# Two parts of an x transform run back to back, and the next layer's second half of products after them

## The reference

```
for i in range(4):
    x1 = _fourier_layer(v, W1, W2)      # rfft2, 24 x 12 modes mixed over 32 channels, irfft2
    x2 = einsum('bcxy,cd->bdxy', v, w_w[i]) + w_b[i]
    v = x1 + x2
    v = (v - mean) * rsqrt(var + eps) * bn_g + bn_b    # mean, var over images and pixels
    if i < 3: v = relu(v)
out = einsum('bcxy,cu->bxyu', v, q_w) + q_b
```

## Time and profile before

| | us |
|---|---|
| median of 3 runs (1403.99, 1404.17, 1419.41) | 1404.17 |
| the profiled execution | 1414.87 |
| its span, first to last instruction | 1413.1 |
| PE busy | 1179.3 |
| DVE busy | 874.0 |
| ACT busy | 540.1 |

### The profile page before, as it was taken

The page is one execution under the profiler, slowest core; times in us unless marked ns, Lnnn a source line. Parts: engine busy times, 40 slices in busy tenths (PEclk is TensorE's granted clock), DMA queues, the critical chain, the costliest instruction groups (busy, mean ns, idle before and its releaser), DMA issues.

```text
span 1413.1 us, 40446 instructions
## 1 busy us (share of the span) xinstructions
PE 1179.3 (83%) x18183; PEld 675.8 (48%) x18183; DVE 874.0 (62%) x1036; ACT 540.1 (38%) x781; POOL 358.5 (25%) x513
## 2 busy tenths in 40 slices
PE   3659899999969999899996998889898877964597
PEld 3434455555544455455554444455455453224562
DVE  6547477677648557576664856657756662058664
ACT  1125345445434434444443543444444462010150
POOL 6382242020326313202032621320202251100000
PEclk9779799999989999999998999999999998985788
DMA  6259998897516999999972699999988065932001
GB/s 158 58 159 222 247 287 202 211 222 185 143 46 181 225 325 366 323 324 319 343 213 62 170 231 328 351 321 308 327 287 273 19 250 200 396 135 51 2 0 31
DMA packets 160086, 300.28 MB, mean 213 GB/s; under 512 B 32552, under 2 KB 104632, under 8 KB 142980
## 3 DMA queue, kind: packets, MB, share of 16 engines
q1 hardware_dynamic: 137754, 254.78, 59.8%
q0 software_dynamic: 19904, 42.18, 10.8%
q10 hardware_dynamic: 2256, 0.75, 0.2%
HBM read 147.86 MB, written 128.48 MB: 196 GB/s over the span
## 4 chain that ended last, share of the span: by engine, by line
PE 63%; DVE 12%; DMA 9%; ACT 6%; issue 4%; SPq 4%; POOL 0%; ACTq 0%; DVEq 0%
PE ps L1589 15%; PE ps L1628 12%; PE ps L1651 7%; PE ps L1663 7%; PE ps L1552 4%; PE ps L1519 4%; PE ps L1614 3%; PE ps L1530 3%; SPq L1045 2%; DMA arena<-half_inverse 2%; DMA maps<-arena 1%; ACT arena L1404 1%; PE ps L1505 1%; DVE ps L1879 1%; DMA half_inverse<-arena 1%
## 5 line engine op out<-in xcount | busy, mean ns | idle before, releaser
L1079 POOL DMA_DIRECT2D arena<-arena x207 | 121.4, 594 | 545.4 <-ACT arena L1421 544.2
L1628 PEld LDWEIGHTS ps<-arena 48*128 48x128 f32 x3072 | 191.9, 198 | 94.6 <-issue 84.1
L1628 PE MATMUL ps<-arena 48*128 48x128 f32 x3072 | 212.6, 290 | 14.6 <-DMA arena<-half_inverse 7.2
L1404 ACT ACTIVATE arena<-ps,arena 128x1024 f32<-128x1024 f32 x96 | 112.3, 1203 | 232.5 <-PE ps L1628 195.0
L1413 ACT ACTIVATE ps<-ps 128x1024 f32<-128x1024 f32 x144 | 145.5, 1011 | 112.1 <-PE ps L1589 111.9
L2035 DVE STREAM_TRANSPOSE arena<-ps 128x1024 f32<-128x1024 f32 x96 | 177.3, 1932 | 1.2 <-PE ps L1651 1.2
L1589 PE MATMUL ps<-arena 32*32 32x512 f32 x2944 | 157.3, 616 | 3.4 <-issue 2.7
L1651 PE MATMUL ps<-arena 32*32 32x512 f32 x3072 | 153.6, 615 | 6.8 <-DVE arena L2022 3.4
L2022 DVE STREAM_TRANSPOSE arena<-arena 128x2048 f32<-128x2048 f32 x64 | 144.1, 2290 | 21.5 <-issue 12.7
L1663 PE MATMUL ps<-arena 128*64 128x96 f32 x2304 | 126.7, 262 | 32.6 <-DVE arena L2035 29.5
L1663 PEld LDWEIGHTS ps<-arena 128*64 128x64 f32 x2304 | 106.9, 145 | 88.3 <-issue 48.6
(11 more groups left out here) (314 smaller groups left out, 1405.3 us busy)
## 6 DMA issues: line engine op xcount, KB each, us to landing
arena<-half_inverse SPq DMA_DIRECT2D x90, 384.0 KB, 10.2
half_inverse<-arena SPq DMA_DIRECT2D x132, 256.0 KB, 4.7
maps<-arena SPq DMA_DIRECT2D x112, 256.0 KB, 4.2
maps<-inputs SPq DMA_DIRECT2D x112, 256.0 KB, 8.9
arena<-maps SPq DMA_DIRECT2D x28, 1024.0 KB, 13.8
maps<-arena SPq DMA_DIRECT2D x28, 1024.0 KB, 9.9
inputs<-maps SPq DMA_DIRECT2D x28, 1024.0 KB, 13.5
arena<-in_mode_w POOLq DMA_DIRECT2D x48, 384.0 KB, 7.1
```

The lines of the kernel that those rows point to most:

```text
L1079: eng.dma_start(dst, src).then_inc((modes_st[batch % 2], last_st, late_st)[part], 16)
L1404: nc.scalar.activation(half(h_out(l, q), h)[:, 1024 * pair:1024 * pair + 1024], ps[:, 2 * pair:2 * pair + 2, :].rearrange("p b n -> p (b n ...
L1628: last = nc.tensor.matmul(ps[:, b, at:at + 128], gtile[s][rows, 4 * b + 2 * h + n, :], iy[rows, :], start=False, stop=(i >= 2 and n == 1))
```

## The change

In each round of a pass TensorE runs the two parts of the x transform one behind the other, and then the second half of the next layer's products. ScalarE copies out in the same order. What is computed is the same.

```
@@ ScalarE
                     if q:
                         modes_evac(l, q - 1, 0)
+                        modes_evac(l, q - 1, 1)
                         square(l, q - 1, 1)
-                        modes_evac(l, q - 1, 1)
@@ TensorE
                     if q:
                         x_transform(l, q - 1, 0)
+                        x_transform(l, q - 1, 1)
                         next_set(l, q - 1, 1)
-                        x_transform(l, q - 1, 1)
```

## The result

The changed kernel took 1468.41 us (median of 4 runs, 1463.93 to 1473.12). The kernel before took 1407.91 us (4 runs). The ratio is 1.042, 95% interval [1.034, 1.049]: 4.2% slower. The forecast was slower, by 42 us; by the ratio it became some 59, and 1468.41 lies above the top of the range (1459). The kernel before was run again beside the experiments and had medians of 1416.74 us (23 runs) and 1414.10 us (17 runs); against these the change costs 52 to 54 us. The profiled execution took 1473.12 us, with a span of 1471.3 us.

What follows compares the result with a forecast made beforehand. The prediction took rounds to be bound by a ring through TensorE and ScalarE's squares. Terms of +47.9, -10 and +4.5 summed to +42.4 us, on the median of 1404.17 a forecast of 1446.6 us, range 1427 to 1459.

Steps and rivals of the forecast that it cites:

- The ring (step 1): Full rounds: TensorE waits for ScalarE's squares, no longer covered by x part 1; +1.14 us in 42 rounds, +47.9 us.
- One term put at nothing: Round q = 15 of each pass: the y transform waits for VectorE's turned map anyway, so the change costs 0.
- rival B: TensorE's clock falls in the new gaps of every round, 2.82 us more each, 118 us in all; 1565 us, chance 0.04.
- Layers 1 and 2 (step 2): Rounds of layers 1 and 2: stops in some 18 of 28 swallow half of the new wait, -10 us.
- the stops: TensorE's instruction supply in layers 1 and 2: standstills without a semaphore, one of 3.79 us, hide new wait, -10 us.
- Rival A: Layers 1 and 2 are paced from outside the round's waits; only layer 0 and pass ends pay, +20.5 us, chance 0.14.
- The end of a pass (step 3): Last round of each pass: ScalarE issues its transfers behind its squares, delaying the mix; +1.5 us each, +4.5 us.

Runs made afterwards that it cites:

- e4: Changed kernel with ScalarE's squares of the second half over one bank of each pair instead of two; 1415.27 us, ratio 1.000 to the kernel before.
- e7: Kernel before with the squares of half 1 over one bank of each pair instead of two; 1395.67 us, measured once.
- e1: Changed kernel with 12 unneeded matmuls (24 rows) added behind the second half of the next layer's products; 1472.79 us, ratio 1.040 to the kernel before.
- e5: Changed kernel with one unneeded matmul of 512 columns (2 rows) behind the second half of the next layer's products; 1451.02 us, ratio 1.025 to the kernel before.
- e9: Kernel before, with ScalarE copying 1024 columns into unread banks before the squares of half 1; 1460.23 us beside 1419.75 for the kernel before, once each.
- e6: Kernel before with the new order on both engines in layers 1 and 2 alone; 1434.78 us, ratio 1.015 to the kernel before.
- e2: Kernel before with the new order on both engines in the last round of each pass alone (q = 16); ratio 0.995 to the kernel before.
- e8: Kernel before with the new order on both engines in the last two rounds of each pass (q = 15 and 16); ratio 0.997 to the kernel before.

## Why the prediction was wrong

- **The ring (step 1) was right in mechanism and near in size.** Forecast 6.72 us from x0 to L1628 and +1.14 a round, measured 6.57 and +0.99. Most of the difference is the pair of x parts: as one row of 48 they take 2.13 us start to start, not 2 x 1.14. Forty-two rounds make 41.6 us instead of 47.9. e4 and e7 show the squares as the cause. One term put at nothing was 0.55 us: in the round with q = 15 the y transform waited for the copy of part 1, which ended 4.76 us after x0 (399.67 + 0.39 - 395.30), 0.10 us before it began, and not for the turned map; the changed kernel gives that back in each pass.
- **The step that failed is the one on the clock, rival B.** I treated it as all or nothing: 1565 us with a chance of 0.04, and nothing for it in the forecast's sum ("the clock of layer 0's window stays at 1.00"). The argument was that gaps of 0.5 us had done nothing and that only 3.83 us had. Between these ends the truth was in the middle: the new stretch makes the clock fall in some rounds, not in each. In layer 0 this cost 16.8 us. Filling the stretch (e1, e5) takes nearly all falls away in the new order; making one (e9) brings them in the old. In layer 0 some 41 us at the lower level cost 16.6 us, 0.4 us for each; layers 1 and 2 have 27 us more at it than before, by this price some 11 us. That makes 28 us for the falls. That the 16.8 us of layer 0 come near the miss of the spans (58.2 - 42.4 = 15.8 us) is chance, since the other terms of the sum are off too and partly cancel. The price of a fallen round was luck as well: 2.82 us were forecast with x0, x1 and next_set slowed, and 2.8 measured, but in those rounds these ran at full speed, and the convolution, L1628 and the y transform behind the stretch were slow. e5, mostly without falls, is at 1451 us, inside the range.
- **Layers 1 and 2 (step 2) came out near the forecast, partly because two terms cancel.** +22 us were forecast (17.2 and 18.1 us a round); it was +33.1 in the profiled execution (17.99 and 18.12), and +21 in e6's runs, some +27 without the gain of two ends. In e5, nearly without the new falls, their windows are 11.8 and 1.4 us longer than before where the ring alone asks for 28 x 0.99 = 27.7. Of the missing 14.5 us some 6 are that e5 has 14 us less at the lower level than the kernel before; the other 9 may be swallowed by the stops, beside the 10 estimated. From the changed kernel's trace the same working gives 27.7 + 11 - 33.1 = 6. With 9 us between executions of one order this is an estimate and not shown. Rival A, a pace set from outside, is not excluded as a part of this in layer 2, where e5 is only 1.4 us longer.
- **The end of a pass (step 3) had the wrong sign.** I let ScalarE's transfers wait for its squares, as they stand behind them in the program. They don't: its queue issues them while the squares run. Forecast +4.5 us, measured -2.1, -2.6 and -2.1 us at the three ends. With 0.55 us in each round before them this is -8.4 us; all that lies outside the windows is -5.6 us.
- In sum, with the forecast in brackets: 41.6 for the ring (47.9), about +28 for the falls (0), about -6 for the stops (-10), -5.6 for the rest (+4.5): 58 us (42.4). On the medians the miss is 1468.41 - 1446.6 = 21.8 us. The part of it beyond 15.8 comes from the medians: the forecast stood on a median of three runs, 1404.17, below each later median of the kernel before.

The Trainium skill (TensorE: Matmul & The Clock Gate, section A second HAM failure mode: psum-queue depth-cycling) tells of frequent small idles between groups of matmuls that made a kernel's clock swing; I gave that a chance of 0.04. e9 and e5 bear it out here (clock 0.94 and 0.99 in layer 0, against 1.00 before and 0.92 in the changed kernel), and e4, at 1.00 with idles of 0.89 us, shows that not each such idle does it. The Trainium skill's statement that instruction fetch is hidden (Runtime: NRT & Kernel Launch, section Instruction fetch mechanics) doesn't hold here as it stands: TensorE stops for up to 4.6 us at the borders of its instruction packets in e1's layer 2. And e1 and e5, which fill the same time with 24 and with 2 rows, differ by 28 us in layers 1 and 2 of one execution each, and by 1.5% of the time of the kernel before over their runs.

## What to carry to other kernels

Work that a stage does for itself, between two uses of the same buffers, is what hides the reader of those buffers; before two such pieces are joined, ask what covers the reader then. Where no buffer is waited for behind them, as in the last rounds here, joining them cost nothing, and in the changed kernel's trace the ends gained 8.4 / 3 = 2.8 us a pass. And when a change opens an idle stretch on TensorE, price its clock as something that happens in a part of the rounds, even where shorter gaps were harmless; the windows of a stage show it, an undisturbed round doesn't.

## What the runs showed of the hardware

- With an idle stretch of 0.73 to 0.84 us (e9) or 1.31 us (the change) in rounds of 16.3 us the clock fell to its lower level in five (e9) and seven (the change) of the fourteen rounds of layer 0, at up to 2.8 us each. With 0.89 us and a shorter second wait (e4) it fell in none. With the old order (the kernel before, e2, e6, e8), whose longest stretch without a matmul in these rounds is 0.5 us, it never fell there. One useless matmul of 512 columns in the stretch left one fall instead of seven (e5).
- ScalarE's DMA issue runs ahead of its own compute: it came at 442.53, 0.17 us after the start of one square and 0.84 us before the start of another, which both stand before it in the program.
- TensorE's stops without a semaphore stand a multiple of 254 of its rows apart (e1, layer 2), and one packet of its instruction queue came per 254 rows. With the DMA engines near 0.9 busy, e1's 22 matmul rows more a round went with 28 us more in layers 1 and 2; in layer 0, at 0.77, with none.
